# A Mamba block and a mixture of experts on one core: the first batch reordered, three small products made one

## The reference

```
z     = layernorm(x)                       # per batch and row of 256
xc    = causal_conv4(in_proj_w @ ctx)      # 256 channels, 4 taps
u     = silu(xc + conv_b)
dt_lo, Bm, Cm = x_proj_w @ u               # 8 + 16 + 16 rows
delta = softplus(dt_proj_w @ dt_lo + dt_proj_b)
state = state * exp(delta * A) + delta * u * Bm      # over 256 steps, 16 states
y     = (sum over states of state * Cm + D * u) * silu(z)
x     = x + y
h     = layernorm(x)                       # per token
x     = x + shared(h) / 2 + sum over experts of gate * expert(h)
```

## Time and profile before

| what | value |
|---|---|
| median of 3 runs | 470.36 us (469.03 to 472.33) |
| the profiled execution | 472.6 us, of which the span of the records is 470.8 us |
| busy TensorE, VectorE, ScalarE, GpSimd | 393.0, 335.5, 245.1, 156.5 us |
| mean granted clock of TensorE | 0.953 |
| DMA | 36.37 MB, mean 77 GB/s |
| chain that ended last | TensorE 50%, VectorE 29%, waiting for nothing shown ("issue") 15%, ScalarE 3% |

### The profile page before, as it was taken

The page is one execution under the profiler, slowest core; times in us unless marked ns, Lnnn a source line. Parts: engine busy times, 40 slices in busy tenths (PEclk is TensorE's granted clock), DMA queues, the critical chain, the costliest instruction groups (busy, mean ns, idle before and its releaser), DMA issues.

```text
span 470.8 us, 7824 instructions
## 1 busy us (share of the span) xinstructions
PE 393.0 (83%) x2610; PEld 345.0 (73%) x2610; DVE 335.5 (71%) x633; ACT 245.1 (52%) x536; POOL 156.5 (33%) x115
## 2 busy tenths in 40 slices
PE   1447655999788999799779999899778999999996
PEld 0225434878668898688668897787667998999996
DVE  3399965769999654679999565589999565444443
ACT  4565521885463253775553344765553354656662
POOL 0455450301455420202464321202474312544442
PEclk9998775899998999999999999899999999999999
DMA  5333474012121223112121224112121223333220
GB/s 185 89 89 90 131 208 166 15 54 80 55 59 38 85 60 113 52 60 67 45 68 45 67 62 129 46 45 67 45 68 48 63 77 92 87 78 86 88 67 24
DMA packets 18882, 36.37 MB, mean 77 GB/s; under 512 B 2082, under 2 KB 4898, under 8 KB 18756
## 3 DMA queue, kind: packets, MB, share of 16 engines
q1 hardware_dynamic: 18852, 36.04, 26.3%
HBM read 34.98 MB, written 1.05 MB: 77 GB/s over the span
## 4 chain that ended last, share of the span: by engine, by line
PE 50%; DVE 29%; issue 15%; ACT 3%; DVEq 1%; DMA 1%; SPq 0%; ACTq 0%
PE acc L401 21%; DVE bu L666 10%; DVE bu L658 7%; PE z L421 6%; PE z L423 6%; PE z L422 6%; DVE stage L741 3%; PE gb L430 3%; DVE pr L677 2%; DVE hl L753 1%; PE bb L340 1%; PE misc L335 1%; DVE cv L604 1%; PE cc L331 1%; PE misc L366 1%
## 5 line engine op out<-in xcount | busy, mean ns | idle before, releaser
L557 ACT ACTIVATE stage<-z,par 128x256 f32<-128x256 f32 x188 | 78.9, 470 | 143.5 <-PE z L423 143.3
L421 PE MATMUL z<-xh,w1l 128*128 (+1 forms) x376 | 117.5, 312 | 10.5 <-DVE stage L743 7.5
L810 POOL TENSOR_TENSOR w2l<-w,w2h 128x512 fp32r<-128x512 f32 (+1 forms) x51 | 68.7, 1350 | 146.0 <-ACT w2h L564 146.0
L422 PE MATMUL z<-xl,w1h 128*128 (+1 forms) x376 | 108.1, 288 | 0.0
L423 PE MATMUL z<-xh,w1h 128*128 (+1 forms) x376 | 108.0, 287 | 0.0
L741 DVE TENSOR_TENSOR stage<-stage,gb 128x512 f32<-128x512 f32 x88 | 59.9, 684 | 64.9 <-ACT stage L557 64.8
L792 POOL TENSOR_TENSOR ya<-ya,pr 128x512 f32<-128x512 f32 x42 | 55.6, 1345 | 121.9 <-DVE pr L677 121.9
L666 DVE TENSOR_TENSOR_SCAN bu<-dA,bu 128x256 f32<-128x256 f32 x128 | 84.4, 720 | 3.4
L421 PEld LDWEIGHTS z<-xh,w1l 128*128 128x128 f32 x376 | 73.1, 194 | 16.3 <-DVE stage L743 9.2
L401 PE MATMUL acc<-stage,w 128*128 128x256 f32 x348 | 82.1, 379 | 0.0
L422 PEld LDWEIGHTS z<-xl,w1h 128*128 128x128 f32 x376 | 73.4, 195 | 0.8
(11 more groups left out here) (116 smaller groups left out, 514.1 us busy)
## 6 DMA issues: line engine op xcount, KB each, us to landing
w<-in_w SPq DMA_DIRECT2D x92, 256.0 KB, 2.7
stage<-in_w SPq DMA_DIRECT2D x11, 512.0 KB, 3.6
selg<-in_selg SPq DMA_DIRECT2D x1, 1056.0 KB, 8.0
x<-in_xT SPq DMA_DIRECT2D x4, 256.0 KB, 4.3
out<-x SPq DMA_DIRECT2D x4, 256.0 KB, 2.6
xr<-in_xr SPq DMA_DIRECT2D x1, 768.0 KB, 10.0
w<-in_w SPq DMA_DIRECT2D x4, 128.0 KB, 2.1
stage<-in_w SPq DMA_DIRECT2D x1, 384.0 KB, 3.8
```

What stands on the lines that cost most here:

```text
L421: pe.matmul(z[p % 2][:, i, :], w1l[:, t, one], xh_, start=k == 0, stop=False)
L422: pe.matmul(z[p % 2][:, i, :], w1h[:, t, one], xl_, start=False, stop=False)
L557: ins = act.activation(hg[:, p % 4, i, :], z[p % 2][:, i, :], ACT.Relu, bias=b1[:, t:t + 1])
L810: pool.tensor_tensor(w2l[:, p % 4, 0:n, :], w2[:, p % RING, 0:n, :], w2h[:, p % 4, 0:n, :].bitcast(F32), ALU.subtract).then_inc(S["w2l_don ...
```

## The change

Five things are edited.

1. **The order in the prologue.** `cv0` to `u`, `xdt`, `dtl`, `dt`, `split` and `sp` come ahead of `stats`; `delta`, `rs1` and `nb1` follow; `zsig` stands behind chunk 0 and `zmul` behind chunk 1. The scratch tile of the sigmoid, `ez`, is `cv` in place of `du`, for which `zsig` waits for `u_done`.
2. **One product in place of two.** `xdt` makes all 104 rows in `misc`: rows 0 to 95 are B and C three times, rows 96 to 103 are dt_lo. The step `xbc` is gone in all batches. dt_proj_w moves from the tensor `small` into `par`, on partitions 96 to 103, with 256 columns.
3. **In the later batches** `zsig` comes after pair 4, behind `dtl`, in place of after pair 3.
4. **softplus in batch 0:** the ReLU part `v` is made by VectorE (add, then max with 0) once ScalarE's |x| is done.
5. **D times u in batch 0** is a product of TensorE with a diagonal matrix `diagd`, which opens the sum in `acc`; `x1` then is one product with `sz` and one addition, both in halves.

```diff
-for ... ("cb", KD), ("xbc", KD * 3 * 2 * NS), ("xdt", KD * DR), ("dtb", KD),
+for ... ("cb", KD), ("xall", KD * NXA), ("dtw", DX), ("dtb", KD),      # NBC = 96, NXA = 104
-         ("usig", 3), ("u", 3), ("xdt", 4), ("dtl", 4), ("zsig", 3), ("zmul", 5), ("dt", 5), ("xbc", 5), ("split", 5), ...
+         ("usig", 3), ("u", 3), ("xdt", 4), ("dtl", 4), ("zsig", 4), ("zmul", 5), ("dt", 5), ("split", 5), ...
-PROLOGUE = ["xin", "stats", "rs1", "cv0", "nb1", "zsig", "taps", "econv", "uclip", "usig", "u", "xdt", "dtl", "xbc", "dt",
-            "zmul", "split", "sp", "delta"] + [n for n, _ in CHUNKS + BACK]
+PROLOGUE = ["xin", "cv0", "taps", "econv", "uclip", "usig", "u", "xdt", "dtl", "dt", "split", "sp", "stats", "delta", "rs1",
+            "nb1", CHUNKS[0][0], "zsig", CHUNKS[1][0], "zmul"] + [n for n, _ in CHUNKS[2:] + BACK]
-        small = sb("small", [NR + NSH, 2 * DX])
+        small = sb("small", [NR + NSH, DX])
-        dtw = small[0:DR, 0:DX]
+        dtw = pv("dtw")[NBC:NXA, :]
-        ez = du
+        ez = cv
 # TensorE
-                                       start=c + k + j == 0, stop=c == NC - 1 and j == 1, skip_group_check=True)
+                                       start=False, stop=c == NC - 1 and j == 1, skip_group_check=True)
...
                         if type(b) is int:
                             pe.wait_ge(ld_sel, 16)
+                            pe.wait_ge(S["v_done"], 1)
                         pe.wait_ge(S["bcs_done"], b + 1)
                         pe.wait_ge(S["sp_done"], b + 1)
...
-                        mm = pe.matmul(cc[0:DR, 0, :], xdt[:, k, :], u[:, k, :], start=k == 0, stop=k == KD - 1)
-                    mm.then_inc(S["dtlo_done"], 1)
-                elif name == "xbc":
-                    for k in range(KD):
-                        mm = pe.matmul(misc[0:96, 0, :], xbc[:, k, :], u[:, k, :], start=k == 0, stop=k == KD - 1)
-                    mm.then_inc(S["xbc_done"], 1)
+                        mm = pe.matmul(misc[0:NXA, 0, :], xall[:, k, :], u[:, k, :], start=k == 0, stop=k == KD - 1)
+                    mm.then_inc(S["xall_done"], 1)
...
                     if first(name, b):
+                        if c == 0:
+                            pe.wait_ge(S["diag_done"], 1)
+                            for k in range(KD):
+                                pe.matmul(acc[:, k, :], diagd[:, k, :], u[:, k, :], start=k == 0, stop=False,
+                                          skip_group_check=True)
 # ScalarE
                     act.wait_ge(S["zz_done"], b + 1)
+                    act.wait_ge(S["u_done"], b + 1)
...
-                    act.wait_ge(S["dtlo_done"], b + 1)
-                    act.activation(dtl, cc[0:DR, 0, :], ACT.Copy).then_inc(S["dtl_done"], 1)
+                    act.wait_ge(S["xall_done"], b + 1)
+                    act.activation(dtl, misc[NBC:NXA, 0, :], ACT.Copy).then_inc(S["dtl_done"], 1)
...
-                    me.then(ins)
+                    ins.then_inc(S["abs_done"], 1)
+                    act.wait_ge(S["abs_done"], b + 1)
                     me.did(act.activation(sp[:], sp[:], ACT.Exp, scale=-1.0))
-                    for k in range(KD):
-                        act.activation(v[:, k, :], bb[:, k, :], ACT.Relu, bias=dtb[:, k:k + 1])
+                    if not first(name, b):
+                        for k in range(KD):
+                            act.activation(v[:, k, :], bb[:, k, :], ACT.Relu, bias=dtb[:, k:k + 1])
 # VectorE, step u
+                        for k in range(KD):
+                            ins = dve.tensor_scalar(diagd[:, k, :], ident, dd[:, k:k + 1], None, ALU.mult)
+                        ins.then_inc(S["diag_done"], 1)
 # VectorE, a new step sp, and delta
+                elif name == "sp":
+                    if first(name, b):
+                        dve.wait_ge(S["abs_done"], 1)
+                        for k in range(KD):
+                            ins = dve.tensor_scalar(v[:, k, :], bb[:, k, :], dtb[:, k:k + 1], 0.0, ALU.add, ALU.max)
+                        ins.then_inc(S["v_done"], 1)
...
                     dve.wait_ge(S["sp_done"], b + 1)
+                    if first(name, b):
+                        dve.wait_ge(S["v_done"], 1)
 # VectorE, step x1
-                    ysum = acc if first(name, b) else y
-                    for k in range(KD):
-                        me.did(dve.scalar_tensor_tensor(y[:, k, :], u[:, k, :], dd[:, k:k + 1], ysum[:, k, :], ALU.mult,
-                                                        ALU.add))
-                    me.wait()
-                    me.then(dve.tensor_tensor(y, y, sz[:], ALU.mult))
-                    dve.tensor_tensor(x1[:, b % 2], y, x1[:, b % 2], ALU.add).then_inc(S["x1_done"], 1)
+                    if first(name, b):
+                        for k in range(KD):
+                            me.did(dve.tensor_tensor(y[:, k, :], acc[:, k, :], sz[:, k, :], ALU.mult))
+                        me.wait()
+                        me.did(dve.tensor_tensor(x1[:, 0, 0], y[:, 0, :], x1[:, 0, 0], ALU.add))
+                        dve.tensor_tensor(x1[:, 0, 1], y[:, 1, :], x1[:, 0, 1], ALU.add).then_inc(S["x1_done"], 1)
+                    else:
...                                                     # as before
```

More of the change, by code:

```diff
@@ L31 @@
 NW = -(-NT // WCH)
+NBC = 3 * 2 * NS
+NXA = NBC + DR
 PAR = {}
 _at = 0
-for _name, _n in (("win", DX), ("cw", KD * KC), ("cb", KD), ("xbc", KD * 3 * 2 * NS), ("xdt", KD * DR), ("dtb", KD),
+for _name, _n in (("win", DX), ("cw", KD * KC), ("cb", KD), ("xall", KD * NXA), ("dtw", DX), ("dtb", KD),
                   ("alog", KD * NS), ("dd", KD), ("rw", KD * NR), ("rb", NR), ("b1", NT), ("ident", P)):
@@ L46 @@
 FRONT = [("xin", 0), ("cv0", 0), ("stats", 0), ("taps", 0), ("rs1", 1), ("econv", 1), ("nb1", 1), ("uclip", 1),
-         ("usig", 3), ("u", 3), ("xdt", 4), ("dtl", 4), ("zsig", 3), ("zmul", 5), ("dt", 5), ("xbc", 5), ("split", 5), ("sp", 5),
+         ("usig", 3), ("u", 3), ("xdt", 4), ("dtl", 4), ("zsig", 4), ("zmul", 5), ("dt", 5), ("split", 5), ("sp", 5),
          ("delta", 5)]
@@ L106, in xattn_ffn_kernel @@
         epsc = sb("epsc", [P, 1])
+        diagd = sb("diagd", [P, KD, P])
         st6 = sb("st6", [P, KD, 6])
@@ L125, in xattn_ffn_kernel @@
         x1 = sb("x1", [P, 2, KD, L])
-        bcr, bcm, dtl = dA[0:96, 0, 0:L], dA[0:96, 1, 0:L // 2].bitcast(BF16), rec[0:DR, 0, :]
+        bcr, bcm, dtl = dA[0:96, 0, 0:L], dA[0:96, 1, 0:L // 2].bitcast(BF16), rec[NBC:NXA, 0, :]
         v, sp = rec, e1
@@ L453, in _ @@
         def _(act):
[L454 removed]
+            me = Steps(act, act_step, 6)
             act.preload_act_table_set("natural_log_exp_and_others")
@@ L684, in step @@
                     dve.wait_ge(ld_xT, b * 16 + 16)
-                    ysum = acc if first(name, b) else y
-                    for k in range(KD):
-                        me.did(dve.scalar_tensor_tensor(y[:, k, :], u[:, k, :], dd[:, k:k + 1], ysum[:, k, :], ALU.mult,
-                                                        ALU.add))
-                    me.wait()
-                    me.then(dve.tensor_tensor(y, y, sz[:], ALU.mult))
-                    dve.tensor_tensor(x1[:, b % 2], y, x1[:, b % 2], ALU.add).then_inc(S["x1_done"], 1)
+                    if first(name, b):
[5 more added lines that the diff above has]
+                    else:
+                        for k in range(KD):
+                            me.did(dve.scalar_tensor_tensor(y[:, k, :], u[:, k, :], dd[:, k:k + 1], y[:, k, :], ALU.mult,
+                                                            ALU.add))
+                        me.wait()
+                        me.then(dve.tensor_tensor(y, y, sz[:], ALU.mult))
+                        dve.tensor_tensor(x1[:, b % 2], y, x1[:, b % 2], ALU.add).then_inc(S["x1_done"], 1)
                 elif name == "centre":
@@ L852 @@
     put("win", xa["in_proj_w"].T)
-    put("xbc", np.concatenate([xp[:, :, DR:]] * 3, axis=2))
-    put("xdt", xp[:, :, :DR])
+    put("xall", np.concatenate([xp[:, :, DR:]] * 3 + [xp[:, :, :DR]], axis=2))
+    par[NBC:NXA, PAR["dtw"][0]:PAR["dtw"][1]] = xa["dt_proj_w"].T
     put("cw", halves(xa["conv_w"]))
@@ L863 @@
     put("ident", np.eye(P, dtype=f32))
-    small = np.zeros((NR + NSH, 2 * DX), f32)
-    small[:DR, :DX] = xa["dt_proj_w"].T
-    small[:NR, DX:] = ff["rb2"]
-    small[NR:, DX:] = ff["sb2"]
+    small = np.zeros((NR + NSH, DX), f32)
+    small[:NR] = ff["rb2"]
+    small[NR:] = ff["sb2"]
     expert = np.arange(NR * HID) // HID
```

12 lines of the change are left out of this document (5 added, 7 removed).

## The result

The changed kernel took 473.62 us (median of 17 runs, 471.08 to 475.59), the kernel before 471.52 us (17 runs, 469.03 to 472.65) beside it on the same chip. The ratio is 1.0048 with a 95% interval of 1.0032 to 1.0065: 2.1 us slower, where 2.65 us faster was forecast. The sign is wrong, and the time lies outside the range of the prediction. The profiled execution took 473.19 us, its span 471.4 us, its mean granted clock 0.957.

A forecast was written before the change was run, and what follows sets the result against it. No engine bounds the whole: a chain of single operations bounds batch 0's front, VectorE its chunks, TensorE the loop's first lap. Batch 0's -2.95 plus 0.3 gives -2.65: 467.7 us from 470.36; own range 466.3 to 469.5, wider 464.0 to 472.0.

The forecast's parts named there:

- Part 1: Batch 0's front: the first tap runs ahead of the statistics and starts at 5.63, -1.99 us.
- Part 2: Batch 0's front: one merged product in place of two between u and the dt product's end, -1.26 us.
- parts 3 and 4: Batch 0 ahead of chunk 0: softplus and statistics +0.03 us, then nb1 on VectorE +0.18; chunk 0 starts at 21.80.
- Part 5: Batch 0's chunks: zsig behind chunk 0 hidden with 0.4 us to spare; zmul in VectorE's full row, +0.71.
- Part 6: Batch 0's x1: D times u on TensorE, hidden, leaves x1 1.71 us instead of 2.33, -0.62.
- Part 7: DMA: par's larger second load costs 0, with bounds 0 and +1 us.
- Rival D: Batch 0's back: last sum and layernorm products run at the high clock, up to 3 us off, 464.7; chance 0.10.
- Part 8's queue: Batches 1 to 3: ScalarE's queue with zsig replaces split's wait for the removed product, +0.1 us each, +0.3.
- Part 8's clock: Batches 1 to 3: no clock fall from TensorE's 1.4 us stop ahead of chunk 0's B, 0 us.
- rival B: Batches 1 to 3: the clock falls behind each new gap, 3 x 1.7 = 5.2 us on top, 472.9; chance 0.12.
- Rivals A and C: A: TensorE gains the removed product in later batches, 464.1, chance 0.13; C: ScalarE holds the prologue, 470.7, chance 0.13.

The follow-up runs named there:

- e10: Changed kernel with stats, rs1 and nb1 back around cv0 in the prologue, as before the change; 473.62 us, ratio 1.0044.
- e2: Kernel before with one edit: zsig after pair 4, behind dtl, in batches 1 to 3; 471.62 us, ratio 1.0006.
- e7: Kernel before with six one-column memsets on VectorE in batch 0's step u, shifting the loop's code; 471.37 us, ratio 0.9997.
- e4: Changed kernel with w1's piece at softplus skipped by ScalarE and GpSimd and done in batch 0's back; 472.92 us, ratio 1.0029.
- e3: Changed kernel with batch 0's zmul between chunk 2's multiplication with B and its scan; 473.39 us, ratio 1.0043.
- e9: Changed kernel: zsig after pair 3, zmul inside chunk 2, w1 piece moved behind x1, stats ahead of sp, ten memsets; 466.89 us, ratio 0.9916.
- e1: Changed kernel with zsig back after pair 3 in batches 1 to 3; 471.11 us, ratio 1.0002.
- e6: Changed kernel with TensorE making the 96 B and C rows again behind dt in batches 1 to 3, unread; 472.86 us, ratio 1.0035.
- e11: Changed kernel with ten memsets on VectorE in batch 0 and the removed products redone, unread, in later batches; 472.72 us, ratio 1.0034.
- e8: Changed kernel with ten one-column memsets on VectorE in batch 0's step u, shifting the loop's code; 472.72 us, ratio 1.0028.

## Why the prediction was wrong

**Parts 1 and 2 came out to 0.1 us in this pair of profiles.** Part 1 was worth nothing by itself: e10 puts its 1.41 us back and chunk 0 gets earlier. Part 2's 1.26 us hold only against this one profile of the kernel before. There the dt product (L340) took 2.07 us; in e2 and e7, whose front is the same, it took 1.13 and 1.17, the high level of the clock:

```profile
18.42 1.13 PE L340 MATMUL bb<-rec,small 8*128 8x256 f32 x4
```

In all ten kernels with the new front, which have one product less ahead of it, it took 2.07. From the end of `u` to the end of the dt product the changed kernel needs 4.70 us, the kernel before 5.97 in its profile, but 5.03 in e2 and 5.06 in e7: a gain of 0.33 to 0.36. That the missing product is what keeps the clock low there was not separated. The landing of `x`, which the expectation for e10 held responsible, is not it: the first tap started at 7.52 in e2 and 7.89 in e7, where the profile before has 7.62.

**The step between parts 3 and 4 failed: chunk 0 at 23.44, not 21.80.** The forecast let `du` keep its 0.7 without a word, and used GpSimd's row only to time a load. Three VectorE operations of this profile with both inputs in SBUF started beside a GpSimd piece, and all ended behind it: `du` by 0.55 us, `zmul` by 0.54, the half addition by 0.29. Those that read PSUM (`bu`, the products with C, `v`) ran beside it at full length. e4, e10, e3 and e9 show it by moving either side. The Trainium skill, "SBUF — State Buffer", section "SBUF: two separate sides", says that VectorE and GpSimd share one pair of ports, which is an exclusive lock: a VectorE operation with two SBUF inputs and one of GpSimd don't share it, the second waits for the whole of the first. The traces agree, and by that rule the price could have been worked out ahead. The kernel before showed it too, in the timeline that the forecast was read from:

```profile
18.07 2.34 POOL L773 TENSOR_TENSOR w1l<-stage,w1h 128x1024 fp32r<-128x1024 f32 x1 [0.64 <-ACT w1h L462]
...
19.54 1.02 DVE L625 CAST dA<-dA 96x256 bf16<-96x256 f32 x1
```

That cast, which has only one input, takes 0.29 in the laps, and chunk 0's scan, started beside a piece, 3.15 where the others take 2.44. The chain was hit once, for 0.71; the change moved chain and pieces by different amounts, so that now `du` was hit, for 2.08.

**Part 5 failed twice**, by the same cause. `zmul` put 1.82 us into VectorE's row (33.48 to 35.30), not 0.71. And the 0.4 us to spare ahead of chunk 1's scan were -0.38: ScalarE ended `zsig` 5.6 us behind chunk 0's start, as forecast (5.7), but chunk 0's scan, now clear of GpSimd, took 2.44, so VectorE was there 0.7 sooner. Together: 1.82 + 0.38 - 0.71 = 1.49, against the 1.43 by which the chunks grew.

**Part 6**: 0.18 of the 0.62 came, since half of an addition lay beside GpSimd (1.03 for 0.42). e9 brings both halves back to 0.42.

**Part 7's 0 held**: nothing up to `u` waited for a later load.

**Rival D came in this pair, and not reliably.** 1.92 us in batch 0's back are the clock's, and hid the loss ahead of it. The code alone doesn't decide it: e1, with the same batch 0, has 3.78 for the last sum. Over the profiles it took 1.99 or 2.00 in seven of the ten kernels with the new front and 3.78 in three (e1, e3, e4), and 3.04, 3.62 and 3.68 with the old one. So the new front may bring the high level more often, but what decides it was not found. The prediction took 3.04 for the low level and half of it for the high one; the rows show 3.78 and 1.99.

**Part 8's queue** was right in kind and too small: +0.41 instead of +0.1. By e2 the place alone costs 0.05; the rest is the merged product, the copy and `zsig` behind it, all three longer, for a reason that stays open.

**Part 8's clock failed, and rival B is half of the answer.** "I take no fall from a stop of 1.4 us between full stretches" was the step. The stop became 1.68, and 4 of 5 laps that could fall behind it did. B asked for a fall in two of three laps; what comes in addition is nearer to 0.8 of a lap (two laps, half of which have their fall already, four in five of the rest), at 1.55 us a fall; this is an estimate from the counts above. The Trainium skill, "TensorE: Matmul & The Clock Gate", section "Why this matters for your kernels", warns against idle gaps between bursts of products, but only against longer ones than this; the measured 4 of 5 decide here. What else the two groups of kernels have in common was not varied, except in e6 and e11, which shorten the stop alone and had no such fall in the one lap each that could have one.

**Outside every part and rival: the place of the code**, 0.32 us a lap, which e8 takes away without touching the loop.

**Rivals A and C** did not come: TensorE cashed nothing in, and chunk 0 was released by `du`, with `nb1` done (`rs1` at 20.85).

The account against the kernel before, from the marks in the profiles. For batch 0 the mean of the kernel before, e2 and e7 stands for before (they differ by up to 1 us), and the mean of the changed kernel, e1, e6, e8 and e11 for after:

| term | us |
|---|---|
| batch 0: first product of the feed-forward layer at 78.40 for 79.67 | -1.3 |
| ScalarE's queue in three laps, 3 x 0.37 | +1.1 |
| the place of the code in three laps, 3 x 0.32 | +1.0 |
| added falls of the clock, 0.8 x 1.55 | +1.2 |
| sum | **+2.0** |
| measured | **+2.1** |

That the sum meets the measured time so closely is partly luck. One low last sum more or less among the five moves the first term by 0.4. For the code's place e8, e9 and e11 stand, and by one amount of shift. The clock's term is worked out from counted laps, and the refill experiments didn't confirm it in the median (-0.76 in e6, 0.0 in e11), so its size stays open. By the same terms e1 should have given back 3.2 us (0.66 a lap in the queue, and the 1.2 of the clock) and gave 2.5.

The one pair of profiles misleads for three reasons. Its before has the latest start of chunk 0 of the three (24.86, for 24.23 in e7 and 23.81 in e2), by the level of the clock in the dt product. Its after has the fast last sum. And laps differ by their falls. Against the mean of the three starts (24.30) the forecast's 21.80 would have been 2.5 us earlier, not 3.06, and the last scan of the changed kernel (60.84) is not level with the one before but 0.6 us late (60.27 is the mean of the three).

## What to carry to other kernels

Before a chain is moved on VectorE, lay GpSimd's timeline beside it: the same 0.69 us multiplication costs up to 2.77 when it starts under a piece, and an edit that is right step by step can deliver the chain into one. Place GpSimd's pieces where VectorE works on operands in PSUM, or where it waits. Time gained ahead of a full engine's row is worth only what is left at the end of that row, so measure it there (here: the last scan), and look for an equal loss before explaining a small total. Profile the kernel before more than once ahead of a forecast: here one operation of its front took 2.07 us in one profile and 1.13 in the next.
